# Two attention layers on one core: the shift cut as columns, a whole-array product in the last two stages, and the parts of attn and v spread over three engines

## The chip, the cores and the metric

One core of one Trainium2 chip. The time is device microseconds of one execution, and lower is better. Engines: PE (matmul), DVE (vector), ACT (activation), POOL (GpSimd), and SP, which only issues DMAs here.

## The reference

Two self-attention layers over x of 4 images, 128 channels and 1024 positions (32 x 32). For each image of each layer:

```python
q = Wq @ x + bq            # 16 x 1024
k = Wk @ x + bk            # 16 x 1024
v = Wv @ x + bv            # 128 x 1024
attn = softmax(q.T @ k, over the last axis)     # 1024 x 1024
x = gamma * (v @ attn.T) + x
```

The second layer takes the output of the first. Everything is fp32.

## The kernel before

A **stage** is one image in one layer: stages 0 to 3 are the four images of layer 0, and 4 to 7 those of layer 1. Stage s + 4 needs the x of stage s. All stages run the same steps, overlapped:

- **QK.s** (`project_qk`, L502): PE projects q and k, three copies over one another, into a ring tile. DVE makes two operations of it, `mask` (L403) and `stack` (L410): in `qk` some copies hold the rounded fp32r value and one the rest, so that one fp32r pass over 64 rows gives q.k closely. SP then copies the halves of `qk` crosswise into `qk_swapped` (`swap`, L265). Stage 0 starts from fp32 q and k directly (`qk_raw`).
- **E.s.i** (L525): a tile of 128 rows of q.T @ k, 1024 wide, as two matmuls on the upper and the lower 64 rows of the array at once. DVE takes the negated row maximum (`max`, L433), and ACT makes exp(e - max) with the row sum (`sum`, L341).
- **The shift** -(max + ln(sum)) belongs to each row. ACT copies the maxima and takes the logarithm (`log_sums`, L347). PE transposes both with two fp32 products (`transpose_shift`, L540), DVE splits the result into a rounded row and the rest (`shift_to_rows`, `rows`, L438), and SP writes these rows into `qk` and `qk_swapped` by two DMAs (`place`, L271). Stage 0 does this in two halves of four tiles, the others once.
- **ET.s.k** (L550): the transposed energies with the shift already in them, and ACT's exp of them is the finished `attn` (L356).
- **Parts.** fp32 x fp32 on PE costs more than fp32r passes do. For six of the eight tiles k (1 to 6), `attn` is cut into `attn_hi` (rounded to fp32r) and `attn_lo` (the rest), and likewise `v` into `v_hi` and `v_lo`. Tiles 0 and 7 are native: fp32 as it is.
- **V.s** (L514) projects v, DVE adds the bias (`v32`, L418).
- **Product** out = v @ attn: PH.s.k is v_hi and v_lo times attn_hi (four passes), PV.s.k is v_hi times attn_lo (two passes) or the native product. Each pass is a pair of matmuls (`add_product`, L564) on 64 rows of the array each: the upper rows write bank 0 of `out_psum`, the lower ones bank 1. k below 4 makes the first 512 positions, the others the second 512. `finish` (L455) adds both banks with gamma onto x, in two DVE operations for each half, and only then may the next half use the banks (`wait_for_out`, L574).

PSUM holds `out_psum` and a ring of three tiles, which raw, QK, E, shift, ET and V share. The order of every engine's work is written out by hand as lists of names (PE_ORDER, L34, and the like), whose last number on PE is the ring tile. A semaphore wait stands ahead of each use, so an engine stops at an item that isn't ready, and all behind it waits too. Where PE would idle, `warm` products of zeros stand. An attn slot k is free once the earlier stage's `lo` of this k is made (or its product, for native tiles).

Who does what before: POOL makes all 48 `lo` and 32 of the `hi`, ACT 16 `hi` and all 8 `v_hi`, DVE all 8 `v_lo`.

Of the kernel before, what the change touches and what calls it, by code (L numbers as in the profile page):

```python
# [72 lines left out]
rows.1.1 mask.3.0 max.2.0 stack.3.0 finish.0.0 max.2.7 max.2.1 max.2.5 max.2.3 v_lo.1.0 max.3.7 max.3.5 finish.0.1
v32.2.0 max.3.1 max.3.4 rows.2.1 max.3.3 max.3.0 mask.4.0 stack.4.0 finish.1.0 max.3.2 max.3.6 v_lo.2.0 max.4.4
max.4.7 finish.1.1 rows.3.1 max.4.3 max.4.6 mask.5.0 stack.5.0 max.4.0 max.4.5 max.4.2 max.4.1 finish.2.0 max.5.0
v32.3.0 max.5.1 v_lo.3.0 finish.2.1 rows.4.1 max.5.5 max.5.7 max.5.2 max.5.3 max.5.4 finish.3.0 mask.6.0 stack.6.0
v32.4.0 v_lo.4.0 max.5.6 max.6.3 finish.3.1 v32.5.0 rows.5.1 max.6.0 max.6.7 max.6.5 max.6.1 finish.4.0 v_lo.5.0
# [595 lines left out]
```

## Time and profile before

| | us |
|---|---|
| median of 3 runs | 207.81 (207.34 to 209.48) |
| profiled execution | 206.91 |
| its span | 205.0 |
| PE busy | 192.7 (94%) |
| ACT busy | 161.0 (79%) |
| POOL busy | 155.9 (76%) |
| DVE busy | 144.8 (71%) |

PE's busy time is from modelled ends, which overlap the next matmul; starts tell more. One slice of forty is 5.1 us. The granted clock is 1.0 (2.4 GHz) in most of the span; in slices 4 and 5 it is 0.8 and 0.5.

### The profile page before, as it was taken

The numbers are of one execution on the slowest core, as the hardware profiler recorded it, in microseconds if no ns is written. First come the engines' busy times: TensorE is split into PE (matmuls) and PEld (weight loads), VectorE is DVE, ScalarE is ACT, GpSimd is POOL, SyncE is SP. The second block draws the span as 40 slices with busy tenths as digits, with TensorE's granted clock in tenths as the row PEclk, the third lists the DMA queues.
The fourth block names the chain that finished last, engine by engine and source line by source line (L and its number), as shares of the span: only waits on it lengthen the run. The fifth ranks groups of instructions, "written<-read, shape, count | busy, mean of one in ns | idle before, by whom it ended". The sixth has DMA issues, their size and how long they took to land.

```text
span 205.0 us, 3349 instructions
## 1 busy us (share of the span) xinstructions
PE 192.7 (94%) x1217; PEld 124.8 (61%) x1217; DVE 144.8 (71%) x146; ACT 161.0 (79%) x237; POOL 155.9 (76%) x88
## 2 busy tenths in 40 slices
PE   7999999999889998999999999999999899998792
PEld 2433254555578656647875867775676768777570
DVE  0297688996999789689866897879874876532202
ACT  2229659889999989997999979699979997558420
POOL 1330000686499999998978988999999999999990
PEclk9998599999999999999999999999999999999998
DMA  6808000030040004002100004001410101001011
GB/s 184 328 14 205 0 2 3 13 93 0 3 106 0 2 6 102 0 6 51 51 3 3 0 2 107 0 6 51 102 53 5 51 0 51 30 28 51 3 51 51
DMA packets 3746, 9.31 MB, mean 45 GB/s; under 512 B 532, under 2 KB 916, under 8 KB 3732
## 3 DMA queue, kind: packets, MB, share of 16 engines
q1 hardware_dynamic: 3732, 9.12, 15.0%
q8 instruction: 10, 0.16, 0.3%
q14 instruction: 4, 0.03, 0.1%
HBM read 2.69 MB, written 2.10 MB: 23 GB/s over the span
## 4 chain that ended last, share of the span: by engine, by line
PE 51%; ACT 15%; POOL 15%; DVE 9%; issue 6%; DMA 2%; SPq 0%; POOLq 0%; DVEq 0%; ACTq 0%
PE out_psum L570 20%; POOL attn_lo L310 10%; PE ring L535 8%; ACT ring L344 7%; ACT attn L362 6%; PE out_psum L600 5%; POOL attn_hi L305 4%; PE out_psum L571 4%; DVE neg_max L435 4%; PE ring L521 4%; PE ring L511 3%; PE ring L556 3%; DMA qk_swapped<-qk 2%; PE ring L499 2%; DVE x_all L460 1%
## 5 line engine op out<-in xcount | busy, mean ns | idle before, releaser
L310 POOL TENSOR_TENSOR attn_lo<-attn,attn_hi 128x1024 fp32r<-128x1024 f32 x48 | 116.2, 2441 | 8.9 <-ACT attn_hi L369 8.0
L435 DVE TENSOR_REDUCE neg_max<-ring 128x1 f32<-128x1024 f32 x64 | 76.5, 1220 | 14.3 <-PE ring L537 13.5
L344 ACT ACTIVATE ring<-ring,neg_max 128x1024 f32<-128x1024 f32 x64 | 69.7, 1088 | 13.1 <-DVE neg_max L435 12.4
L362 ACT ACTIVATE attn<-ring 128x1024 f32<-128x1024 f32 x64 | 63.5, 1024 | 15.8 <-PE ring L558 15.4
L305 POOL TENSOR_SCALAR attn_hi<-attn 128x1024 fp32r<-128x1024 f32 x32 | 36.2, 1138 | 27.9 <-ACT attn L362 27.4
L556 PE MATMUL ring<-qk,qk_swapped 64*128 64x512 f32 x64 | 30.1, 485 | 2.7 <-ACT attn L362 2.0
L570 PE MATMUL out_psum<-attn_hi,v_hi 64*128 64x512 f32 x96 | 30.7, 399 | 1.5 <-DVE x_all L463 1.2
L571 PE MATMUL out_psum<-attn_hi,v_hi 64*128 64x512 f32 x96 | 30.7, 399 | 0.0
L558 PE MATMUL ring<-qk_swapped,qk 64*128 64x512 f32 x64 | 30.5, 491 | 0.0
L570 PE MATMUL out_psum<-attn,v 64*128 64x512 f32 x64 | 30.0, 588 | 0.0
L571 PE MATMUL out_psum<-attn,v 64*128 64x512 f32 x64 | 30.0, 588 | 0.0
L571 PE MATMUL out_psum<-attn_hi,v_lo 64*128 64x512 f32 x96 | 29.6, 388 | 0.0
L570 PE MATMUL out_psum<-attn_hi,v_lo 64*128 64x512 f32 x96 | 29.6, 388 | 0.0
L570 PE MATMUL out_psum<-attn_lo,v_hi 64*128 64x512 f32 x96 | 28.2, 400 | 0.1
L571 PE MATMUL out_psum<-attn_lo,v_hi 64*128 64x512 f32 x96 | 28.2, 400 | 0.0
L535 PE MATMUL ring<-qk_swapped,qk 64*128 64x512 f32 x56 | 24.7, 445 | 2.4 <-ACT attn L362 2.2
L460 DVE SCALAR_TENSOR_TENSOR x_all<-out_psum,weights,x_all 128x512 f32<-128x512 f32 x16 | 12.0, 748 | 20.2 <-PE out_psum L571 20.2
L537 PE MATMUL ring<-qk,qk_swapped 64*128 64x512 f32 x56 | 25.0, 448 | 0.0
L556 PEld LDWEIGHTS ring<-qk,qk_swapped 64*128 64x128 f32 x64 | 11.7, 184 | 14.0 <-issue 12.6
L570 PEld LDWEIGHTS out_psum<-attn_hi,v_hi 64*128 64x128 f32 x96 | 17.0, 184 | 5.0 <-issue 2.7
L570 PEld LDWEIGHTS out_psum<-attn_lo,v_hi 64*128 64x128 f32 x96 | 17.5, 184 | 3.5 <-POOL attn_lo L310 1.0
L570 PEld LDWEIGHTS out_psum<-attn_hi,v_lo 64*128 64x128 f32 x96 | 17.7, 184 | 2.3
(48 smaller groups left out, 322.4 us busy)
## 6 DMA issues: line engine op xcount, KB each, us to landing
qk_swapped<-qk SPq DMA_DIRECT2D x16, 256.0 KB, 3.7
out_dram<-x_all SPq DMA_DIRECT2D x8, 256.0 KB, 2.0
x_all<-x_in SPq DMA_DIRECT2D x3, 512.0 KB, 7.1
x_all<-x_in SPq DMA_DIRECT2D x2, 256.0 KB, 3.2
late<-late_in SPq DMA_DIRECT2D x1, 448.0 KB, 6.3
weights<-weights_in SPq DMA_DIRECT2D x1, 132.0 KB, 2.1
qk<-shift_rows SPq DMA_DIRECT2D x7, 8.0 KB
qk_swapped<-shift_rows SPq DMA_DIRECT2D x7, 8.0 KB
```

The source lines that it names most:

```text
L305: nc.gpsimd.tensor_scalar(attn_hi[:, k - 1], attn[:, k], 1.0, 0.0, ALU.mult, ALU.add).then_inc(hi_made["gpsimd"], 1)
L310: nc.gpsimd.tensor_tensor(attn_lo[:, k - 1], attn[:, k], attn_hi[:, k - 1].bitcast(fp32), ALU.subtract).then_inc(lo_made, 1)
L344: nc.scalar.activation(e[:], e[:], ACT.Exp, bias=max_column(s, i), accum_out=row_sum[s][:, i:i + 1]).then_inc(sum_made, 1)
L362: nc.scalar.activation(attn[:, k], ring_tile("ET", s, k)[:].rearrange("p (a n) -> p a n", a=2), ACT.Exp).then_inc(attn_made, 1)
L435: nc.vector.tensor_reduce(max_column(s, i), ring_tile("E", s, i)[:], axis=AX.X, op=ALU.max, negate=True).then_inc(max_made, 1)
L460: nc.vector.scalar_tensor_tensor(out=to, in0=out_psum[:, 0:HALF], scalar=gamma, in1=x_all[:, s, part], op0=ALU.mult, op1=ALU.add).then_inc ...
L535: nc.tensor.matmul(to[:, 0:HALF], q_over_k[0:deep, rows], k_over_q[0:deep, 0:HALF], start=True, stop=True)
L537: nc.tensor.matmul(to[:, HALF:N], k_over_q[64:64 + deep, rows], q_over_k[64:64 + deep, HALF:N], start=True, stop=True).then_inc(e_mm, 1)
L556: nc.tensor.matmul(to[:, 0:HALF], k_over_q[0:64, first], q_over_k[0:64, part], start=True, stop=True)
L558: nc.tensor.matmul(to[:, HALF:N], q_over_k[64:128, second], k_over_q[64:128, part], start=True, stop=True).then_inc(et_mm, 1)
L570: nc.tensor.matmul(out_psum[:, 0:HALF], v[0:64], a[0:64], start=start, stop=stop)
L571: last = nc.tensor.matmul(out_psum[:, HALF:N], v[64:128], a[64:128], start=start, stop=stop)
```

## The change

- **Shift.** `log_sums` makes only the logarithm of 4 or 8 sums; the copy of the maxima goes. A new DVE item `parts` (`cut_shift`) makes three small operations of 128 x 4 or 128 x 8 in SBUF: shift = neg_max - log_sum, its rounded value, and the rest. PE transposes these 8 or 16 columns by one fp32r product with a unit matrix. `rows` is one DVE copy out of PSUM. SP's two DMAs stay as they are. `ADDED`, a way without these DMAs, is empty: its branches run in no stage; only two POOL memsets of 128 x 128 remain of it.
- **Product.** In stages 6 and 7 (`WHOLE`) each pass is one matmul on all 128 rows, which writes the bank of its half; `finish` is then one DVE operation a half, and a half waits only for the same bank's last finish.
- **Stage 1's stack** goes from DVE to ACT (`evac`) and POOL (mask and stack from SBUF).
- **Parts:** POOL 38 `lo`, 32 `hi`, 6 `v_hi`, 6 `v_lo`; ACT 16 `hi`, 2 `v_hi`; DVE 10 `lo` (two in stage 3, one in 5, three in 6, four in 7) and 2 `v_lo`.
- **Loads:** `late` has 5 tiles of 64 KB instead of 7. A new load `units` of 5 such tiles stands ahead of the last two x, and POOL rounds it (one operation of 128 x 640).
- **All five orders are new.** PE has 26 `warm` instead of 31.

```diff
+WHOLE = (6, 7)
+FROM_SBUF = (1,)
...
 PE_ORDER = """
-raw.0.0.0 raw.0.1.1 QK.1.0.2 E.0.2.0 E.0.1.1 warm.0.8 E.0.0.2 E.0.3.0 warm.0.2 E.0.4.1 warm.0.1 E.0.5.2 E.0.7.0
-warm.0.2 E.1.6.1 warm.0.3 E.1.4.2 warm.0.3 shift.0.0.0 warm.0.2 E.1.7.1 warm.0.1 E.0.6.0 V.0.0.2 ET.0.3.1 warm.0.1
...
+raw.0.0.0 raw.0.1.1 QK.1.0.2 E.0.1.0 E.0.3.1 E.0.6.2 warm.0.4 E.0.0.0 E.0.2.1 E.0.5.2 warm.0.2 E.0.4.0 warm.0.1
+V.0.0.1 shift.0.0.2 warm.0.2 E.0.7.0 E.1.7.1 QK.2.0.2 warm.0.4 ET.0.2.0 warm.0.1 ET.0.3.1 warm.0.3 E.1.3.0 ET.0.1.2
...
+shift.7.1.0 PV.6.0 ET.6.7.1 ET.6.4.2 ET.6.1.0 PH.6.5 PH.6.3 PV.6.2 PV.6.5 ET.7.0.2 ET.7.2.0 ET.7.7.1 PH.6.1 PV.6.7
+ET.7.3.2 ET.7.5.0 PV.6.1 PV.6.3 PH.6.4 PH.6.6 ET.7.1.2 ET.7.4.1 ET.7.6.0 PV.6.4 PV.6.6 PH.7.3 PH.7.2 PV.7.7 PH.7.1
+PV.7.2 PV.7.3 PV.7.1 PV.7.0 PH.7.5 PH.7.6 PH.7.4 PV.7.5 PV.7.4 PV.7.6
 ACT_ORDER = """
-sum.0.2 sum.0.1 sum.0.0 sum.0.3 log.0.0 sum.0.4 sum.0.5 sum.0.7 sum.1.6 sum.1.4 sum.1.7 sum.0.6 attn.0.3 log.0.1
...
+evac.1.0 sum.0.1 sum.0.3 sum.0.6 sum.0.0 sum.0.2 sum.0.5 log.0.0 sum.0.4 v_hi.0.0 sum.0.7 sum.1.7 attn.0.2 log.0.1
...
+sum.7.1 attn.5.5 attn.5.7 hi.5.5 sum.7.4 sum.7.7 sum.7.0 attn.6.2 attn.6.5 sum.7.5 log.7.1 attn.6.6 attn.6.0
+attn.6.3 hi.6.3 attn.6.4 attn.6.1 attn.6.7 v_hi.7.0 attn.7.0 attn.7.2 hi.6.6 hi.7.2 attn.7.3 attn.7.7 attn.7.5
+attn.7.1 attn.7.4 hi.7.5 attn.7.6 hi.7.4 hi.7.6
 DVE_ORDER = """
-mask.1.0 max.0.2 stack.1.0 max.0.1 max.0.0 max.0.3 max.0.4 max.0.5 max.0.7 max.1.6 max.1.4 rows.0.0 max.1.7 max.0.6
...
+max.0.1 max.0.3 max.0.6 max.0.0 max.0.2 max.0.5 max.0.4 parts.0.0 v32.0.0 rows.0.0 max.0.7 max.1.7 mask.2.0
...
+parts.7.1 v32.7.0 lo.6.2 rows.7.1 lo.6.1 lo.6.3 finish.6.0 finish.6.1 lo.7.3 lo.7.1 lo.7.6 lo.7.5 finish.7.0
 finish.7.1
 POOL_ORDER = """
...
+mask.1.0 stack.1.0 v_lo.0.0 hi.0.2 hi.0.1 hi.0.3 lo.0.2 lo.0.1 hi.0.6 lo.0.3 lo.0.6 hi.0.5 lo.0.5 hi.0.4 lo.0.4
...
+v_lo.7.0 lo.6.4 lo.6.6 hi.7.3 hi.7.1 lo.7.2 lo.7.4
...
             def log_sums(s, h):
-                act.wait_ge(max_made, all_of(nth_max, s, tiles))
-                nc.scalar.copy(neg[:, len(tiles):], neg[:, 0:len(tiles)]).then_inc(max_twice, 1)
                 act.wait_ge(sum_made, all_of(nth_sum, s, tiles))
-                sums = row_sum[s][:, tiles.start:tiles.stop][:, None, :].to_broadcast([P, 2, len(tiles)])
-                nc.scalar.activation(log, sums, ACT.Ln).then_inc(log_made, 1)
+                nc.scalar.activation(log_sum[s][:, part], row_sum[s][:, part], ACT.Ln).then_inc(log_made, 1)
...
+            def cut_shift(s, h):
...
+                dve.wait_ge(max_made, all_of(nth_max, s, tiles))
+                dve.wait_ge(log_made, nth_log[s, h])
+                nc.vector.tensor_tensor(shift[s][:, part], neg_max[s][:, part], log_sum[s][:, part],
+                                        ALU.subtract).then_inc(shift_made, 1)
+                dve.wait_ge(shift_made, nth_parts[s, h])
+                nc.vector.tensor_copy(hi, whole).then_inc(shift_hi_made, 1)
+                dve.wait_ge(shift_hi_made, nth_parts[s, h])
+                nc.vector.tensor_tensor(lo, whole, hi.bitcast(fp32), ALU.subtract).then_inc(shift_cut, 1)
...
             def shift_to_rows(s, h):
-                nc.vector.tensor_scalar(shift_masked[0:rows], src, columns[0:rows, mask:mask + 1], None,
-                                        ALU.mult).then_inc(shift_masked_made, 1)
-                nc.vector.tensor_tensor(shift_rows[s % 2][0:rows], src, shift_masked[0:rows].bitcast(fp32),
-                                        ALU.subtract).then_inc(shift_in_rows, 1)
+                nc.vector.tensor_copy(rows_of(s, h)[:], ring_tile("shift", s, h)[0:rows, 0:P]
+                                      ).then_inc(shift_in_rows, 1)
...
+            def attn_lo_of(s, k):
+                wait_for_cut(dve, "hi", s, k)
+                nc.vector.tensor_tensor(attn_lo[:, k - 1], attn[:, k], attn_hi[:, k - 1].bitcast(fp32),
+                                        ALU.subtract).then_inc(cut_made["lo", "vector"], 1)
...
             def finish(s, h):
+                if s not in WHOLE:
+                    nc.vector.scalar_tensor_tensor(out=to, in0=out_psum[:, 0:HALF], scalar=gamma, in1=x,
+                                                   op0=ALU.mult, op1=ALU.add).then_inc(x_half_made, 1)
...
+                bank, x = (out_psum[:, part], x) if s in WHOLE else (out_psum[:, HALF:N], to)
...
             def transpose_shift(s, h):
-                nc.tensor.matmul(to, both(neg_max, s, h), late[:, IDENTITY], start=True, stop=False)
-                nc.tensor.matmul(to, both(log_sum, s, h), late[:, IDENTITY + 1], start=False,
-                                 stop=True).then_inc(shift_mm, 1)
+                nc.tensor.matmul(to, parts, units[:, IDENTITY], start=True, stop=True).then_inc(shift_mm, 1)
...
                 for n, (v, a) in enumerate(passes):
...
+                    if s in WHOLE:
+                        last = nc.tensor.matmul(out_psum[:, half_of(k)], v, a, start=start, stop=stop)
```

## Rows read from the trace of the kernel before

**Rows 1.** Stretches: bounds, us, busy us of each engine, granted clock, DMA share, GB/s.

```profile
18.00:26.00 8.00, 8.00 (x23) 2.21 (x21) 5.29 (x5) 6.15 (x13) 0.00 (x0) 0.57 0.23 55
...
38.00:175.00 137.00, 132.49 (x918) 93.27 (x919) 111.53 (x112) 126.99 (x189) 125.52 (x67) 1.00 0.12 32
...
sum 205.00, PE 192.69 PEld 124.75 DVE 144.76 ACT 161.01 POOL 155.92; mean PE 32.12 PEld 20.79 DVE 24.13 ACT 26.84 POOL 25.99
```

**Rows 2.** The chain that ended last, from the page: shares of the span.

```profile
PE 51%; ACT 15%; POOL 15%; DVE 9%; issue 6%; DMA 2%; SPq 0%; POOLq 0%; DVEq 0%; ACTq 0%
```

**Rows 3.** Waits: engine and line, what it waited for, total us, times, longest.

```profile
DVE x_all L460 <- PE out_psum L571: 20.2, 11, 6.6
```

**Rows 4.** Groups by form: busy us, mean ns | idle us ahead of them, releasers.

```profile
L310 POOL TENSOR_TENSOR attn_lo<-attn,attn_hi 128x1024 fp32r<-128x1024 f32 x48 | 116.2, 2441 | 8.9 <-ACT attn_hi L369 8.0
...
L435 DVE TENSOR_REDUCE neg_max<-ring 128x1 f32<-128x1024 f32 x64 | 76.5, 1220 | 14.3 <-PE ring L537 13.5
...
L344 ACT ACTIVATE ring<-ring,neg_max 128x1024 f32<-128x1024 f32 x64 | 69.7, 1088 | 13.1 <-DVE neg_max L435 12.4
...
L362 ACT ACTIVATE attn<-ring 128x1024 f32<-128x1024 f32 x64 | 63.5, 1024 | 15.8 <-PE ring L558 15.4
...
L305 POOL TENSOR_SCALAR attn_hi<-attn 128x1024 fp32r<-128x1024 f32 x32 | 36.2, 1138 | 27.9 <-ACT attn L362 27.4 <-PE out_psum L571 0.5
...
L369 ACT CAST attn_hi<-attn 128x1024 fp32r<-128x1024 f32 x16 | 16.7, 1046 | 0.2
...
L374 ACT CAST v_hi<-v 128x768 fp32r<-128x768 f32 x8 | 6.6, 829 | 0.0
...
L446 DVE TENSOR_SCALAR shift_masked<-ring,weights 16x128 fp32r<-16x128 f32 x7 | 2.3, 334 | 5.3 <-PE ring L547 5.3
```

**Rows 5.** Timeline of stage 0: start us, us, engine, line, instruction, idle before.

```profile
19.23 0.21 ACT L354 ACTIVATE log_sum<-row_sum 128x8 f32<-128x8 f32 x1
...
26.24 0.39 PE L546 MATMUL ring<-late,neg_max 128*8 128x128 f32 x2
...
31.11 0.50 PE L556 MATMUL ring<-qk,qk_swapped 64*128 64x512 f32 x1
...
31.65 1.02 ACT L362 ACTIVATE attn<-ring 128x1024 f32<-128x1024 f32 x1
...
37.02 2.06 POOL L305 TENSOR_SCALAR attn_hi<-attn 128x1024 fp32r<-128x1024 f32 x2 [25.06 <-ACT attn L362]
```

**Rows 6.** Timeline of POOL and DVE around two `v_lo`.

```profile
123.71 2.41 POOL L310 TENSOR_TENSOR attn_lo<-attn,attn_hi 128x1024 fp32r<-128x1024 f32 x1 [1.72 <-ACT attn_hi L369]
...
124.41 2.53 DVE L430 TENSOR_TENSOR v_lo<-v,v_hi 128x768 fp32r<-128x768 f32 x1 [1.09 <-ACT v_hi L374]
...
140.62 0.95 DVE L430 TENSOR_TENSOR v_lo<-v,v_hi 128x768 fp32r<-128x768 f32 x1
```

**Rows 7.** Timeline of PE from a projection of 128 rows to pairs of 64.

```profile
139.26 1.98 PE L511 MATMUL ring<-x_all,late 128*128 128x512 f32 x4
...
141.18 0.50 PE L556 MATMUL ring<-qk,qk_swapped 64*128 64x512 f32 x1
...
141.51 0.39 PE L570 MATMUL out_psum<-attn_hi,v_hi 64*128 64x512 f32 x1
...
141.75 0.39 PE L570 MATMUL out_psum<-attn_hi,v_hi 64*128 64x512 f32 x1
```

**Rows 8.** Timeline of stage 7's shift on PE, and of V.7.0.

```profile
174.73 0.39 PE L546 MATMUL ring<-late,neg_max 128*16 128x128 f32 x2
...
176.53 2.05 PE L521 MATMUL ring<-late,x_all 128*128 128x128 f32 x16
```

**Rows 9.** Timeline of the end: POOL's last parts, PE's last pair, DVE's last.

```profile
193.12 7.05 POOL L310 TENSOR_TENSOR attn_lo<-attn,attn_hi 128x1024 fp32r<-128x1024 f32 x3
...
200.56 0.39 PE L571 MATMUL out_psum<-attn_lo,v_hi 64*128 64x512 f32 x1
...
201.79 0.75 DVE L463 SCALAR_TENSOR_TENSOR x_all<-out_psum,weights,x_all 128x512 f32<-128x512 f32 x1
```

More of the change, by code:

```diff
@@ L73 @@
[L73 to L77, printed above, removed]
@@ L78 @@
-mask.7.0 stack.7.0 max.6.6 max.6.2 max.6.4 finish.4.1 rows.6.1 v32.6.0 max.7.1 max.7.6 finish.5.0 max.7.4 v_lo.6.0
-max.7.0 max.7.3 finish.5.1 max.7.5 max.7.2 max.7.7 rows.7.1 finish.6.0 v32.7.0 v_lo.7.0 finish.6.1 finish.7.0
+max.0.1 max.0.3 max.0.6 max.0.0 max.0.2 max.0.5 max.0.4 parts.0.0 v32.0.0 rows.0.0 max.0.7 max.1.7 mask.2.0
+stack.2.0 parts.0.1 max.1.3 rows.0.1 max.1.2 max.1.6 max.1.1 max.1.5 max.1.4 max.1.0 max.2.5 parts.1.1 v32.1.0
+max.2.2 rows.1.1 max.2.3 max.2.0 finish.0.0 mask.3.0 stack.3.0 max.2.7 max.2.6 max.2.1 max.2.4 max.3.3 max.3.2
@@ new lines @@
+finish.0.1 v32.2.0 parts.2.1 max.3.4 rows.2.1 max.3.0 max.3.7 mask.4.0 max.3.6 stack.4.0 finish.1.0 max.3.5 max.3.1
+max.4.5 max.4.1 max.4.0 finish.1.1 max.4.4 parts.3.1 max.4.3 rows.3.1 max.4.2 max.4.7 mask.5.0 stack.5.0 max.4.6
+finish.2.0 parts.4.1 v32.3.0 max.5.3 max.5.1 max.5.4 max.5.7 rows.4.1 finish.2.1 v32.4.0 lo.3.1 max.5.0 lo.3.6
+max.5.5 finish.3.0 max.5.2 max.5.6 mask.6.0 stack.6.0 v_lo.4.0 parts.5.1 finish.3.1 v32.5.0 rows.5.1 mask.7.0
+max.6.0 stack.7.0 max.6.1 max.6.4 finish.4.0 max.6.2 max.6.6 max.6.3 max.6.5 v_lo.5.0 max.6.7 finish.4.1 max.7.6
@@ L80 @@
+v32.6.0 parts.6.1 max.7.2 max.7.3 max.7.1 finish.5.0 rows.6.1 max.7.4 max.7.7 max.7.0 lo.5.5 max.7.5 finish.5.1
+parts.7.1 v32.7.0 lo.6.2 rows.7.1 lo.6.1 lo.6.3 finish.6.0 finish.6.1 lo.7.3 lo.7.1 lo.7.6 lo.7.5 finish.7.0
 finish.7.1
@@ L325, in _ @@
                     attn_hi_of(s, k)
+                elif what == "lo":
+                    attn_lo_of(s, k)
+                elif what == "v_hi":
+                    make_v_hi(s)
+                elif what == "v_lo":
+                    make_v_lo(s)
+                elif what == "mask":
+                    mask_from_sbuf(s)
                 else:
-                    attn_lo_of(s, k)
+                    stack_from_sbuf(s)
         @block.scalar
@@ L384, in _ @@
                     make_v_hi(s)
+                elif what == "evac":
+                    evacuate_qk(s)
                 else:
@@ L438, in shift_to_rows @@
             def shift_to_rows(s, h):
-                rows = 2 * len(tiles_of(s, h))
-                mask = HALF_SHIFT_MASK if s in BY_HALVES else SHIFT_MASK
-                src = ring_tile("shift", s, h)[0:rows, 0:P]
+                rows = P if added(s, h) else 2 * len(tiles_of(s, h))
                 dve.wait_ge(shift_mm, nth_shift[s, h])
-                earlier = [use[1:3] for use in DVE_USES if use[0] == "rows" and nth_rows[use[1:3]] < nth_rows[s, h]]
-                if earlier:
-                    dve.wait_ge(shift_in_rows, nth_rows[earlier[-1]])
@@ L476, in _ @@
                     make_v_lo(s)
+                elif what == "lo":
+                    attn_lo_of(s, i)
+                elif what == "parts":
+                    cut_shift(s, i)
                 elif what == "rows":
@@ L653 @@
         late[:, BV + l] = bv_l[None, :]
-    late[:, IDENTITY] = np.eye(P, dtype=f32)
-    late[:, IDENTITY + 1] = -late[:, IDENTITY]
+    units = np.zeros((P, UNITS, P), f32)
+    units[:, IDENTITY] = np.eye(P, dtype=f32)
+    for t in range(SLOTS):
+        for row in (t, SLOTS + t):
+            units[[row, 64 + row], SELECT + t] = 1.0
     late[:, LAYER1] = sets[QK_SETS]
```

307 lines of the change are left out of this document (188 added, 119 removed).

## The prediction

> **What bounds the kernel now.** I read the chain of waits first: PE has 51% of it, ACT and POOL 15% each, DVE 9% [rows 2]. No engine is the bound alone. The busy times say why [rows 1]: from 38 to 175 us, with the clock at 2.4 GHz, ACT is busy for 127.0 of 137.0 us, POOL for 125.5, DVE for 111.5. PE shows 132.5, but modelled ends flatter it, so I count it by starts. A pair of fp32r matmuls of 512 columns starts 0.23 us after the one ahead, a set of four fp32 halves takes 1.92 [rows 7], a V 1.98 [rows 8]. With the counts of the order, E and ET cost 0.23 each, PH 0.92, a cut PV 0.46, a native PV 1.92, QK 1.92, V 1.98, a stage 0 E 0.96, a shift 0.32, a `warm` 0.23. Between the shifts 0.1 (about 37 us) and 7.1 (174.7 us) [rows 8] stand 126.6 us of this, so PE is idle for about 10 us there. All four engines have some 19 us a stage; an engine that is relieved gives back only waits.
>
> **The start** is slack. In stage 0 the logarithm of the first half starts at 19.23, but PE comes to its shift at 26.24, behind E tiles and warm products; the first ET is at 31.11, the first attn at 31.65, POOL's first `hi` at 37.02 [rows 5]. From 18 to 26 us the granted clock is 0.57, mostly the 1.2 GHz level [rows 1].
>
> **The end** is POOL's. After the shift of stage 7 PE has 23.2 us of work and takes 26.2 us for it (174.73 to 200.95) [rows 8, 9]; POOL makes `lo` without a gap until 200.17, the last pair follows, then two halves of a finish. DVE waits 20.2 us in all for PE's products [rows 3].
>
> **The change, part by part.**
>
> *Start.* Log.0.0 now stands behind six sums instead of four: two tiles more at DVE's 1.2 us [rows 4]. DVE loses the mask and stack of stage 1, two operations on a tile, of which I credit one (1.2). So the log ends at about 20.6, `parts` takes 0.5, and shift to ET is 4.9 us as now [rows 5]: ET at 26.0, attn at 26.5, 5.1 us earlier. ACT has 11.9 us behind it then and not 12.2, but 1.1 of it is the new `evac`, so about 1 us is owed: **-4.0**. Stage 1's q and k pass from POOL: rounding the units 0.7, mask 1.0, stack 2.35 (like a `lo`, 7.05/3) [rows 9]. They end some 2 us later than now, ahead of an E.1 first wanted beyond 21: nothing, and 2 us if the cover is gone. The load adds 0.32 MB and `late` loses 0.13 MB: it delays images 2 and 3, not wanted before QK.2; nothing.
>
> *Order on PE.* From shift.0.1 up to shift.7.1 the new order has 124.8 us of PE work instead of 126.6 (three ET and two PH fewer, one V more, among others): **-1.8**.
>
> *Relief of ACT and POOL in the middle.* From the first attn to log.7.1 ACT had 131.9 us and has 121.3: 6 `v_hi` (0.83), the copies, and attn and `hi` moved behind it [rows 4]. POOL has from its first `hi` 38 x 2.35 + 32 x 1.03 + 6 x 0.77 + 5 x 1.76 = 135.7 us (the last two are `hi` and `lo` scaled to 768 columns) instead of 145.8 [rows 5, 9]. PE's 10 us of idle time can shrink by at most this: between 0 and -5 I take **-2.0**, since DVE doesn't get lighter (141.5 to 143.8 without waits).
>
> *Parts on DVE.* The trace shows what DVE pays when both inputs lie in SBUF: `v_lo` takes 0.95 us with POOL between operations and 2.53 when it starts 0.7 us into a `lo` of POOL, which is the rest of that operation and then itself [rows 6]. Ops with one PSUM input (the max, 1.22) don't show this. A `lo` on DVE is 0.95 x 1024/768 = 1.27 plus a rest. The mean rest of POOL's mix is (38 x 2.35² + 32 x 1.03²) / (2 x 122.3) = 1.0 us. Ten make 22.7 on DVE, and hold POOL for 12.7 against 23.5 saved; the six `v_lo` gone give back 5.7. For SBUF the Trainium skill says the same and more (SBUF — State Buffer, section SBUF: two separate sides): the two engines share a port pair under an exclusive lock, and it also binds a DVE copy in a 2-port mode. By that rule the new copy in `parts` would wait as well.
>
> *Shift.* Gone from the chain from log to ET: one ACT copy (0.18, ahead of the log) and one small DVE operation (0.33) [rows 4]; new: three of at most 0.2 us each in `parts`, both ends in SBUF. If they run together behind one rest, 1.0 + 0.5 a stage; if POOL gets in between each time, 1.0 + 2 x 1.76 (POOL's mean operation) + 0.5 = 5.0. No small operation with two SBUF inputs is in the trace, so both ends stay open. I take the one wait, nearest to the `v_lo` rows, and a third of seven of them exposed, since ACT holds 6 to 12 us of other work behind each log: 7 x 1.0 / 3 = **+2.3**, less 0.3 for the lighter transpose: **+2.0**. Queued behind `parts` on DVE are maxima, which ACT's sums and the ring wait for.
>
> *Whole array and tail.* A full-array pass streams the same 512 columns: 1.92/4 for each fp32 half [rows 7]; nothing gained a pass. Changing between 64-row and 128-row work costs 0.1 us: the pair after the switch is followed 0.33 and not 0.24 us later [rows 7]. Stages 6 and 7 have 14 changes instead of 7: +0.7. On such switches TensorEngine Tiling (Array Packing) in the Trainium skill, Tiling Modes, says that a change of mode drains the engine; the trace agrees, at this 0.1. Behind shift.7.1 PE has 26.2 us of work instead of 23.2; POOL has only four operations of stage 7 and is no bound. With 1.5 us idle: 26.2 + 0.7 + 1.5 = 28.4 instead of 26.2, and the last finish is one operation: -0.75 [rows 9]. Together **+1.4**. ACT has 21.1 us behind log.7.1, then two DVE `lo`, PV, finish: about 25, inside it.
>
> **Sum:** -4.0 - 1.8 - 2.0 + 2.0 + 1.4 = -4.4. The profiled execution was 206.91 (its span 205.0 and 1.9 around it): 202.5. The median is 0.9 above: **203.4**.
>
> **Rivals.**
>
> *DVE is held behind POOL (slower).* Place: `parts` in stages 1 to 7. Each costs 5.0, i.e. 4.5 of waiting; a third exposed is 10.5 instead of 2.3, so 203.4 + 8.2 = **211.6**. DVE would be busy for 143.8 + 31.5 + 10 = 185 us of some 190. It decides from about 2.9 us of waiting each: then a third of seven is the 6.7 us that the rest gains. For it: all-busy POOL and the 2.53 row [rows 1, 6]; by the named SBUF page the copy waits too. Against it: DVE's next operation may start before POOL's. Chance 0.18.
>
> *PE has the same work (no change).* In all it has 173.7 us instead of 174.9. If what the start wins is lost later at the ring or in DVE's list, only 1.2 remains: **206.6**. For it: ACT's attn slots are free only when `lo` is made, DVE's `lo` come late in its list, finish.7.0 now stands behind lo.7.5, and the start can fall into the low clock. Chance 0.22.
>
> *The waits go (more gain).* PE's idle in the middle shrinks by 5, no `parts` is exposed: 203.4 - 3 - 2 = **198.4**. Against it: DVE and ACT are fed by the same three ring tiles. Chance 0.13.
>
> *The forecast* has 0.47; its own range is 201 to 206.
>
> **Numbers.** 1% is about 2.1 us, which is what can be told from no change: below 205.7 is faster, above 209.9 slower. Faster: 0.13, 0.42 of the forecast and 0.03 of the no-change case, 0.58. Slower: 0.16 of the rival and 0.03 of others, 0.19. Same: 0.23. The range 198.0 to 210.0 leaves out a tail of the third rival and most of the slower one.
>
> **What would show it.** First attn at 26 to 27 us. `parts` operations: 0.2 us each with one of about 1 us, or several of 1 to 2.4 us. DVE's `lo` at 1.3 to 3.6 us. POOL idle in the last 10 us. PE's pace in stages 6 and 7: a pass each 0.23 us; if 128-row fp32r passes came slower, the 72 cut passes of these stages would add 1.4 us for each 0.02. The prediction is wrong if attn starts no earlier than 30 us, or if DVE is busy for more than 170 us.

## The result: 7.6% slower, and all of it comes with the three small operations of the shift

| | before | after |
|---|---|---|
| median | 207.57 us (4 runs) | 223.63 us (222.56 to 225.16, 4 runs) |
| ratio to before | | 1.0763 [1.0667, 1.0859] |
| profiled execution, its span | 206.91, 205.0 | 223.82, 222.0 |
| PE, ACT, POOL, DVE busy | 192.7, 161.0, 155.9, 144.8 | 196.8, 156.5, 153.5, 171.5 |
| granted clock, mean | 0.978 | 0.939 |

PE and POOL are busy for about as long as before, ACT for 4.5 us less. DVE has 26.7 us more than before. The first view is the page of the kernel after: the granted clock in 40 slices, and the chain that ended last, by engine and by line [rows 2 for before].

```profile
PEclk9995799985999889999999999979999769999999
...
PE 52%; DVE 16%; POOL 13%; ACT 10%; issue 7%; DVEq 0%; ACTq 0%; POOLq 0%
PE out_psum L694 12%; PE ring L645 8%; POOL attn_lo L348 8%; PE out_psum L692 6%; PE ring L621 6%; ACT attn L447 5%; ACT ring L435 5%; DVE shift_parts L544 5%; PE out_psum L728 5%; PE out_psum L695 5%; DVE shift L541 4%; PE ring L669 4%; PE ring L631 3%; DVE neg_max L526 3%; DVE v L511 2%
```

DVE's share rose from 9% to 16%. Two lines on 128 x 8 numbers, L541 and L544, have 9% of the chain, about 20 us. The groups by form say what they cost (mean ns of one behind the busy time):

```profile
L521 DVE TENSOR_TENSOR attn_lo<-attn,attn_hi 128x1024 fp32r<-128x1024 f32 x10 | 20.2, 2049 | 4.8 <-POOL attn_hi L343 4.8
...
L544 DVE CAST shift_parts<-shift 128x8 fp32r<-128x8 f32 x7 | 10.5, 1502 | 0.2
...
L541 DVE TENSOR_TENSOR shift<-neg_max,log_sum 128x8 f32<-128x8 f32 x7 | 9.0, 1289 | 0.6 <-ACT log_sum L442 0.3
...
L546 DVE TENSOR_TENSOR shift_parts<-shift,shift_parts 128x8 fp32r<-128x8 f32 x7 | 4.7, 674 | 0.2
```

The three take 24.2 us in seven stages, from 0.5 us in stage 4 to 5.2 us in stage 1. What they take alone is seen in stage 4, where POOL happens to be idle. The timelines of the kernel after, first DVE's in stages 2 and 4 (start, duration):

```profile
70.07 0.90 DVE L541 TENSOR_TENSOR shift<-neg_max,log_sum 128x8 f32<-128x8 f32 x1
71.01 2.29 DVE L544 CAST shift_parts<-shift 128x8 fp32r<-128x8 f32 x1
73.33 0.75 DVE L546 TENSOR_TENSOR shift_parts<-shift,shift_parts 128x8 fp32r<-128x8 f32 x1
74.00 1.21 DVE L526 TENSOR_REDUCE neg_max<-ring 128x1 f32<-128x1024 f32 x1
...
110.01 0.17 DVE L541 TENSOR_TENSOR shift<-neg_max,log_sum 128x8 f32<-128x8 f32 x1
110.22 0.17 DVE L544 CAST shift_parts<-shift 128x8 fp32r<-128x8 f32 x1
110.42 0.17 DVE L546 TENSOR_TENSOR shift_parts<-shift,shift_parts 128x8 fp32r<-128x8 f32 x1
```

and POOL's over the same two moments:

```profile
66.23 7.03 POOL L348 TENSOR_TENSOR attn_lo<-attn,attn_hi 128x1024 fp32r<-128x1024 f32 x3
73.23 0.84 POOL L354 TENSOR_SCALAR v_hi<-v 128x768 fp32r<-128x768 f32 x1
...
104.43 2.38 POOL L348 TENSOR_TENSOR attn_lo<-attn,attn_hi 128x1024 fp32r<-128x1024 f32 x1
111.42 1.06 POOL L343 TENSOR_SCALAR attn_hi<-attn 128x1024 fp32r<-128x1024 f32 x1 [4.62 <-ACT attn L447]
```

POOL's three `lo` end at 68.59, 70.95 and 73.27, and `v_hi` at 74.07. DVE's three operations end at 70.97, 73.30 and 74.08. So each of them waits for one whole operation of POOL or its rest. The reading, which e5 tests below, is this: in the 0.03 us between two of DVE's, where it waits for its own semaphore, POOL's next operation gets in.

Who waited for whom, in the kernel after:

```profile
POOL attn_hi L343 <- ACT attn L447: 36.3, 11, 10.2
ACT attn L447 <- PE ring L671: 23.6, 16, 5.1
ACT ring L435 <- DVE neg_max L526: 19.0, 15, 4.3
...
PE ring L657 <- DVE shift_parts L546: 5.7, 3, 2.5
```

PE's own wait at the shift is only 5.7 us. The chain that ended last nevertheless goes through the small operations in six of the seven stages, all but stage 4, and leaves them by what stands next in DVE's list: a maximum in stages 2, 3 and 6, V's bias (`v32`) in 1 and 7, a `finish` in 5. The pieces of the chain in stage 2 (start, us, what) show the way by a maximum:

```profile
68.94 1.21 DVE v L511
70.15 0.83 DVE shift L541
...
71.01 2.30 DVE shift_parts L544
...
74.00 1.22 DVE neg_max L526
...
76.26 0.20 ACT ring L435
...
76.60 1.19 PE ring L621
```

DVE is through with `parts` at 74.1, takes the maximum that was queued behind it, ACT takes the sum of that ring tile, and only then is the tile free for PE's next projection.

The span, cut at PE's shifts of stage 0's second half and of stage 7 (us; e1 and e8 are experiments below):

| | start to shift.0.1 | from there to shift.7.1 | to the end | span |
|---|---|---|---|---|
| before | 36.20 | 138.53 | 30.27 | 205.0 |
| after | 32.09 | 159.00 | 30.91 | 222.0 |
| e1, shift as before | 31.72 | 137.32 | 31.46 | 200.5 |
| e8, parts on POOL | 30.93 | 137.37 | 30.90 | 199.2 |

The start is gained, the end is nearly what it was, and the middle has 20.5 us more. In the middle stretch the granted clock is 0.94 in the kernel after and 1.00 in the other three, and PE is busy for 139.0 us with 886 matmuls where e8 needs 130.4 for 888: up to 8.6 us of the loss may be matmuls at the lower clock, which came with the waits.

One profile, of e2, is of a disturbed execution, so only durations of single operations are taken from it.

### The profile page after: what moved, and what is told of

Its sections match the earlier page's. It is cut to its first block, busy times and chain, and to the rows that moved or that the text cites. A ratio compares the mean times of both kernels' runs of the same rounds, so it can differ in the third digit from the quotient of the medians.

```text
span 222.0 us, 3109 instructions
## 1 busy us (share of the span) xinstructions
PE 196.8 (89%) x1095; PEld 123.4 (56%) x1097; DVE 171.5 (77%) x162; ACT 156.5 (71%) x223; POOL 153.5 (69%) x95
## 4 chain that ended last, share of the span: by engine, by line
PE 52%; DVE 16%; POOL 13%; ACT 10%; issue 7%; DVEq 0%; ACTq 0%; POOLq 0%
PE out_psum L694 12%; PE ring L645 8%; POOL attn_lo L348 8%; PE out_psum L692 6%; PE ring L621 6%; ACT attn L447 5%; ACT ring L435 5%; DVE shift_parts L544 5%; PE out_psum L728 5%; PE out_psum L695 5%; DVE shift L541 4%; PE ring L669 4%; PE ring L631 3%; DVE neg_max L526 3%; DVE v L511 2%
## 5 line engine op out<-in xcount | busy, mean ns | idle before, releaser
L348 POOL TENSOR_TENSOR attn_lo<-attn,attn_hi 128x1024 fp32r<-128x1024 f32 x38 | 94.9, 2517 | 3.8 <-ACT attn_hi L453 3.2
L447 ACT ACTIVATE attn<-ring 128x1024 f32<-128x1024 f32 x64 | 63.3, 1026 | 24.4 <-PE ring L671 23.6
L343 POOL TENSOR_SCALAR attn_hi<-attn 128x1024 fp32r<-128x1024 f32 x32 | 33.3, 1049 | 39.3 <-ACT attn L447 36.3
L645 PE MATMUL ring<-qk_swapped,qk 64*128 64x512 f32 x56 | 26.5, 483 | 1.2 <-ACT attn L447 0.4
L647 PE MATMUL ring<-qk,qk_swapped 64*128 64x512 f32 x56 | 26.7, 487 | 0.0
L694 PE MATMUL out_psum<-attn_hi,v_hi 64*128 64x512 f32 x72 | 23.8, 411 | 0.3 <-POOL attn_hi L343 0.3
L521 DVE TENSOR_TENSOR attn_lo<-attn,attn_hi 128x1024 fp32r<-128x1024 f32 x10 | 20.2, 2049 | 4.8 <-POOL attn_hi L343 4.8
L695 PE MATMUL out_psum<-attn_hi,v_hi 64*128 64x512 f32 x72 | 23.8, 411 | 0.0
L694 PE MATMUL out_psum<-attn,v 64*128 64x512 f32 x48 | 23.6, 614 | 0.0
L695 PE MATMUL out_psum<-attn,v 64*128 64x512 f32 x48 | 23.6, 614 | 0.0
L694 PE MATMUL out_psum<-attn_hi,v_lo 64*128 64x512 f32 x72 | 22.9, 398 | 0.0
L695 PE MATMUL out_psum<-attn_hi,v_lo 64*128 64x512 f32 x72 | 22.9, 397 | 0.0
L694 PE MATMUL out_psum<-attn_lo,v_hi 64*128 64x512 f32 x72 | 21.9, 409 | 1.1 <-POOL attn_lo L348 1.1
L669 PEld LDWEIGHTS ring<-qk,qk_swapped 64*128 64x128 f32 x64 | 11.7, 191 | 19.4 <-issue 17.8
L695 PE MATMUL out_psum<-attn_lo,v_hi 64*128 64x512 f32 x72 | 21.9, 408 | 0.0
L360 POOL TENSOR_TENSOR v_lo<-v,v_hi 128x768 fp32r<-128x768 f32 x6 | 11.5, 1922 | 10.9 <-ACT v_hi L458 10.8
L631 PEld LDWEIGHTS ring<-late,x_all 128*128 128x128 f32 x128 | 16.7, 209 | 2.4 <-issue 2.4
L631 PE MATMUL ring<-late,x_all 128*128 128x128 f32 x128 | 17.9, 299 | 0.0
```

The lines of the kernel that those rows point to most:

```text
L343: nc.gpsimd.tensor_scalar(attn_hi[:, k - 1], attn[:, k], 1.0, 0.0, ALU.mult, ALU.add).then_inc(cut_made["hi", "gpsimd"], 1)
L348: nc.gpsimd.tensor_tensor(attn_lo[:, k - 1], attn[:, k], attn_hi[:, k - 1].bitcast(fp32), ALU.subtract).then_inc(cut_made["lo", "gpsimd"], 1)
L447: nc.scalar.activation(attn[:, k], ring_tile("ET", s, k)[:].rearrange("p (a n) -> p a n", a=2), ACT.Exp).then_inc(attn_made, 1)
L631: last = nc.tensor.matmul(to[:, j * C:(j + 1) * C], x_all[:, s, j * P:(j + 1) * P], late[:, WV + layer(s), :], start=True, stop=True)
L645: nc.tensor.matmul(to[:, 0:HALF], q_over_k[0:deep, rows], k_over_q[0:deep, 0:HALF], start=True, stop=True)
L647: nc.tensor.matmul(to[:, HALF:N], k_over_q[64:64 + deep, rows], q_over_k[64:64 + deep, HALF:N], start=True, stop=True).then_inc(e_mm, 1)
```

## The experiments

Four theories stood at first. LOCK: the small operations wait for POOL, and that is the loss. CLOCK: gaps on PE let the granted clock fall, and that costs. ORDER: the new orders cost. WHOLE: the whole-array product costs. The kernel before took 207.59 us beside e1 to e4, 207.41 beside e5 to e8 and 206.99 beside e9 to e12; each ratio is to the one that ran beside.

**e1: the kernel after with the shift of before.** All the rest of the change stays.

```
-                nc.vector.tensor_tensor(shift..., neg_max..., log_sum..., ALU.subtract)
-                nc.vector.tensor_copy(hi, whole)
-                nc.vector.tensor_tensor(lo, whole, hi.bitcast(fp32), ALU.subtract)
+                nc.scalar.copy(neg[:, len(tiles):], neg[:, 0:len(tiles)])     # on ACT
+                (two products on PE, mask and subtraction from PSUM on DVE)
```

> The changed kernel with the shift made as before the change: ACT's copy of the maxima, two fp32 transposes on PE, two DVE operations out of PSUM, and no `parts` on DVE. All orders, the whole-array product and the spread of hi and lo stay as changed. Theory LOCK (the three small DVE operations of `parts` wait for POOL's running operation, 24.3 us of DVE time in stages 1 to 7, and hold the shift and the maxima behind them): at least 13 of the 16 us come back, 206 to 211 us, and ACT, POOL and PE lose most of their idle time in the middle. Rival ORDER (the new lists and the tail are worse by themselves): at most 5 us come back, 218 us or more. Rival WHOLE (128-row passes and their mode changes): as ORDER, with the loss behind the shift of stage 6.

Measured 202.77 us, ratio 0.9791 [0.9745, 0.9837]. The whole loss, 223.63 - 202.77 = 20.9 us, sits in the new shift; the rest of the change is worth 2.1%. That is more than the 13 to 18 us that I had expected back. ACT's waits for DVE's maxima fall from 19.0 to 8.2 us, those for PE from 23.6 to 11.7, and the chain's shares (page) are:

```profile
PE 56%; POOL 25%; ACT 11%; issue 5%; DVE 1%; POOLq 0%; ACTq 0%
```

DVE has left the chain.

**e2: the kernel before with the new shift alone.** `parts` is put into DVE's list of before, in each stage between the logarithm's last maximum and `rows`.

```
+ dve: shift = neg_max - log_sum; hi = copy(shift); lo = shift - hi      (in words)
+ pool: the unit matrix is rounded once
- act: copy of the maxima;  pe: two fp32 products  ->  one fp32r product
```

> The kernel before with the new shift alone: `parts` on DVE one item ahead of `rows` in DVE's list (right ahead of `rows` in stage 7), logarithm without the copy, one fp32r transpose. All else as before. LOCK: the operations wait for POOL here too, some 3 us a stage; 7 stages give 215 to 225 us. ORDER and WHOLE: the shift is not to blame, 207 to 210 us.

Measured 233.1 us, ratio 1.1222 [1.1152, 1.1292]: some 25 us without any of the new orders, and more than the 215 to 225 us expected. The three operations take 6.6, 9.1 and 8.2 us there, 23.9 together. The new orders are not to blame. That they hide a little of the cost (20.9 us in the kernel after) is a guess: `parts` stands in other places of DVE's list here.

**e3: the kernel before with the whole-array product alone.**

```
+WHOLE = (6, 7)
+ if s in WHOLE: last = nc.tensor.matmul(out_psum[:, half_of(k)], v, a, ...)
```

> The kernel before with the whole-array product of stages 6 and 7 alone (one matmul of 128 rows a pass into the bank of its half, one DVE operation for each half of a finish). LOCK: no part in the loss, 206 to 208.5 us: two finishes shorter by 0.75 us on the path at the end, some 0.1 us lost at each change of mode. WHOLE: 211 us or more.

Measured 207.42 us, ratio 1.0 [0.9976, 1.0024]. Neutral, as LOCK had it.

**e4: the kernel after with 12 small products of zeros ahead of PE's wait at the shift** of stages 1 to 7, so that PE is not idle there.

```
+                if s > 0:
+                    for _n in range(12):
+                        nc.tensor.matmul(ring_tile("shift", s, h)[:, 0:HALF], zeros[:, 0:P], zeros[:], ...)
```

> The changed kernel with 12 more products of zeros on PE ahead of the wait for each shift of stages 1 to 7, into the ring tile that the shift owns by then (about 2.8 us of PE time each, where PE mostly waits). Rival CLOCK (the loss is the granted clock, 0.939 instead of 0.978, once PE idles): the clock returns to 0.97 and 4 to 8 us come back, 216 to 219 us. LOCK: the waits stay; the time changes by no more than 3 us either way, since the products also take PE time where it had none to give: 221 to 228 us.

Measured 226.94 us, ratio 1.0948 [1.0905, 1.0991]. Span and granted clock of the core:

```profile
core 0: 225.3 us, clock 0.977
```

The clock is back at the level of before (0.978), and the kernel is still slower than the one after by 3.3 us: the 4 to 8 us that CLOCK promised did not come back. Part of that is the products themselves: 84 at 0.23 us are 19 us of PE, of which only some lie in gaps (DVE's `rows` now wait 11.8 us for PE). So the run does not price the clock, and it shows only that keeping the clock up in this way wins nothing. Where no small operation of DVE waits (e1, e7, e8) the clock is 0.99; that the gaps which DVE makes bring the fall is read from this, and not shown by itself.

**e5: the second operation made from the same inputs as the first,** so that no semaphore wait stands between them.

```
+                nc.vector.tensor_tensor(hi, neg_max[s][:, part], log_sum[s][:, part], ALU.subtract)
-                dve.wait_ge(shift_made, nth_parts[s, h])
-                nc.vector.tensor_copy(hi, whole)
```

> The changed kernel, but the rounded part of the shift is made from neg_max and log_sum by a tensor_tensor of its own, right behind the first one and with no wait between the two; the third operation waits for both. Same number of DVE operations, same values. Theory GAP (POOL's next operation starts in the gap that a semaphore wait leaves between two small DVE operations, and each gap costs one more wait of 1.0 to 2.4 us): the second operation takes 0.2 us, DVE is busy some 8 us less, and a third of the 20.9 us that `parts` costs comes back, 214 to 219 us. Rival EACH (every small operation waits, gap or none): the second still shows about 1.5 us and the time stays at 222 to 226 us.

Measured 216.64 us, ratio 1.0449 [1.0382, 1.0516]: 7.0 us back. DVE's timeline in stage 2 of e5, to set against the one above:

```profile
69.97 0.94 DVE L541 TENSOR_TENSOR shift<-neg_max,log_sum 128x8 f32<-128x8 f32 x1
70.83 0.15 DVE L543 TENSOR_TENSOR shift_parts<-neg_max,log_sum 128x8 fp32r<-128x8 f32 x1
71.08 2.15 DVE L547 TENSOR_TENSOR shift_parts<-shift,shift_parts 128x8 fp32r<-128x8 f32 x1
```

The second operation follows at once and takes 154 ns in the mean of seven instead of 1502; the third, behind a wait, now meets the whole POOL operation and rises from 674 to 1397 ns. POOL's next `lo` starts at 70.83 too and does not hold the second operation up. That one is now a subtraction and not a copy, but the first and the third are subtractions too and do wait. So it is the wait at a semaphore that lets POOL in. DVE was relieved of 4.5 us and not of the 8 expected, since the third operation took over part of the waiting; these 4.5 us gave 7.0 us of time, a third of the 20.9, as expected.

**e6 and e7: the disputed cost by itself.** To e1, three chained small operations are added ahead of `mask` in stages 2 to 7. Nothing of the kernel uses their results. In e6 all inputs are in SBUF; in e7 one input of each is the ring tile in PSUM.

```
+                src = weights[:, 0:8]                    # e6;   e7: ring_tile("QK", s, 0)[:, 0:8]
+                nc.vector.tensor_tensor(small[0][:], src, weights[:, 8:16], ALU.subtract)
+                nc.vector.tensor_copy(small[1][:], small[0][:])          # e7: copies src
+                nc.vector.tensor_tensor(small[2][:], src, small[1][:], ALU.subtract)
```

> The kernel with the old shift and all the rest of the change (202.8 us), plus three small DVE operations of 128 x 8 ahead of each `mask` of stages 2 to 7, chained by waits as in `parts`, on columns of `weights` in SBUF; their outputs go to scratch. They stand on no shift's chain. Theory LOCK: each waits for POOL's running operation; about 3 us a stage of DVE time, 18 in all. If what costs is DVE being held (maxima and sums late), the time goes to 209 to 218 us; if what costs is the late shift alone, it stays below 206 us.

> As the run with small operations in SBUF, in the same places, but the first input of each of the three comes from the ring tile in PSUM, so none has two inputs in SBUF and the copy is from PSUM. LOCK: no waits for POOL; each takes 0.2 to 0.3 us, 5 us of DVE time in all, 202.5 to 205 us. Rival COUNT (it is the number of small chained operations that costs, wherever the inputs lie): the same time as with SBUF inputs.

Groups of e6:

```profile
L512 DVE TENSOR_TENSOR small<-weights,small 128x8 f32<-128x8 f32 x6 | 9.4, 1567 | 0.2
L510 DVE COPY small<-small 128x8 f32<-128x8 f32 x6 | 8.3, 1378 | 0.2
...
L508 DVE TENSOR_TENSOR small<-weights 128x8 f32<-128x8 f32 x6 | 4.5, 752 | 1.0 <-PE ring L628 1.0
```

Groups of e7:

```profile
L510 DVE COPY small<-ring 128x8 f32<-128x8 f32 x6 | 1.0, 166 | 0.2
L512 DVE TENSOR_TENSOR small<-ring,small 128x8 f32<-128x8 f32 x6 | 1.0, 166 | 0.2
L508 DVE TENSOR_TENSOR small<-ring,weights 128x8 f32<-128x8 f32 x6 | 1.0, 162 | 0.9 <-PE ring L628 0.9
```

e6 took 232.99 us, ratio 1.1235 [1.118, 1.1289]; e7 206.33, ratio 0.994 [0.9906, 0.9973]. The same eighteen operations cost 30.2 us over e1 with all inputs in SBUF, and 3.6 us with one in PSUM. In e7 POOL had a `hi` or a `lo` under way beside five of the six groups, and none of the eighteen took over 168 ns. LOCK is shown, away from the chain of the shift, and the number of operations is not what costs. Both sizes were missed: I had expected 209 to 218 and 202.5 to 205. What went wrong is again the exposure: 19.2 us more on DVE (22.2 against 3.0) made 26.7 us of time. By the orders, `mask` and `stack` stand right behind these operations, and the waits of e6 show PE held there:

```profile
PE ring L677 <- DVE qk L521: 15.7, 5, 6.4
...
PE ring L638 <- DVE qk L521: 4.6, 1, 4.6
```

L521 is `stack`. PE waits 20.3 us for it, against 2.1 us in e7. The granted clock is 0.933 in e6 and 0.99 in e7; how much of the 26.7 us is the clock's was not shown.

**e8: the kernel after with the three operations on POOL.** `parts` stands in POOL's list near the place where the logarithm ends.

```
-                nc.vector.tensor_tensor(...)   nc.vector.tensor_copy(hi, whole)   nc.vector.tensor_tensor(...)
+                nc.gpsimd.tensor_tensor(...)   nc.gpsimd.tensor_scalar(hi, whole, 1.0, 0.0, ALU.mult, ALU.add)   nc.gpsimd.tensor_tensor(...)
```

> The changed kernel with the three operations of `parts` made by POOL instead of DVE, in POOL's list behind the operation that runs when the logarithm ends (by the trace of the run with the old shift). LOCK: POOL has no one to wait for but itself; the operations take 0.1 to 0.3 us each, the shift is late by at most the rest of one POOL operation, and the time is 202 to 207 us. ORDER or COUNT: no better than 218 us.

Measured **200.93 us**, ratio 0.9683 [0.9626, 0.974]: faster than before, 22.7 us faster than after, and 1 us below the range expected. Groups of e8 on POOL:

```profile
L393 POOL TENSOR_SCALAR shift_parts<-shift 128x8 fp32r<-128x8 f32 x7 | 2.4, 339 | 0.6
...
L390 POOL TENSOR_TENSOR shift<-neg_max,log_sum 128x8 f32<-128x8 f32 x7 | 1.5, 211 | 0.0
L395 POOL TENSOR_TENSOR shift_parts<-shift,shift_parts 128x8 fp32r<-128x8 f32 x7 | 1.4, 206 | 0.6
```

They cost POOL 5.3 us where they cost DVE 24.2. The middle one is long once, in stage 7 (timeline of e8, POOL then DVE):

```profile
166.71 1.16 POOL L393 TENSOR_SCALAR shift_parts<-shift 128x8 fp32r<-128x8 f32 x1
...
166.59 1.22 DVE L538 TENSOR_TENSOR attn_lo<-attn,attn_hi 128x1024 fp32r<-128x1024 f32 x1
```

Here the wait goes the other way: DVE's `lo` began first and POOL's small copy ends with it.

**e9: e8 with the first shift ahead of V.0.0 on PE, and `rows` ahead of `v32` on DVE.** In the kernel after, V.0.0 takes 3.62 us at the low clock and stands ahead of the shift.

```
-V.0.0.1 shift.0.0.2 warm.0.2 E.0.7.0 ...
+shift.0.0.2 V.0.0.1 warm.0.2 E.0.7.0 ...
```

> `parts` on POOL (200.9 us), and in stage 0 PE's shift.0.0 ahead of V.0.0, DVE's rows.0.0 ahead of v32.0.0. In the changed kernel V.0.0 runs at the low clock level for 3.6 us while the shift waits behind it, and the first attn starts at 29.4 us and not at the 26.5 of the prediction. If that V is what the start lacks: first attn at 26 to 27 us; if this reaches the end, 1 to 2 us come back, 199 to 200 us. If the start is covered by what follows: 200.5 to 201.5 us with the early attn.

Measured 205.26 us, ratio 0.9927 [0.9894, 0.9959]: 4.3 us slower than e8, a miss (199 to 201.5 expected). PE's timeline in e9:

```profile
20.25 0.39 PE L724 MATMUL out_psum<-zeros 128*128 128x512 bf16 x1
22.39 0.26 PE L653 MATMUL ring<-units,shift_parts 128*8 128x128 f32 x1 [1.74 <-POOL shift_parts L395]
22.65 3.75 PE L627 MATMUL ring<-late,x_all 128*128 128x128 f32 x16
...
31.61 0.50 PE L665 MATMUL ring<-qk,qk_swapped 64*128 64x512 f32 x1
```

and of e8:

```profile
20.14 3.24 PE L627 MATMUL ring<-late,x_all 128*128 128x128 f32 x16
23.13 0.30 PE L653 MATMUL ring<-units,shift_parts 128*8 128x128 f32 x1
...
28.07 0.50 PE L665 MATMUL ring<-qk,qk_swapped 64*128 64x512 f32 x1
```

The shift comes 0.7 us earlier, but PE waits for the parts with nothing to do, V starts 2.5 us later, and E.0.7, E.1.7 and QK.2, which stand ahead of the first ET, follow it. The first ET is 3.5 us later, and the first attn starts at 32.15 us and not at the 26 to 27 expected. From 20 to 30 us the clock is 0.66 in place of 0.86. V ahead of the shift was filling a wait.

**e10: e8 with DVE's three `lo` of stages 3 and 5 back on POOL.**

```
 DVE: -lo.3.1 -lo.3.6 -lo.5.5        POOL: +lo.3.1 +lo.3.6 +lo.5.5
```

> `parts` on POOL, and the three `lo` that DVE makes in stages 3 and 5 made by POOL instead, among its other `lo` of the stage. Theory LOCK: a `lo` takes POOL 2.35 us and DVE 1.22 us in which POOL stands too, so each of the three gives POOL some 1.1 us more and DVE 2 us less; POOL is the fullest engine there, so 1 to 3 us slower, 202 to 204 us. Rival: DVE's `lo` and its wait hurt the maxima more, and it gets faster, under 200 us.

Measured 206.65 us, ratio 0.9979 [0.9947, 1.0011]: 5.7 us worse than e8, in the direction expected and more than the 1 to 3 us. From 100 to 120 us POOL is full in both (19.41 and 19.42 us busy), but DVE has 10.14 us of work in place of 18.29, ACT 15.11 in place of 18.29, PE 17.58 in place of 18.92. The granted clock there is 0.91 in place of 1.00, which may be part of the 5.7 us. The likely reading is that everything waits behind the longer queue of POOL. These `lo` on DVE pay, lock and all.

**e11: e8 with all six `lo` of stage 7 on DVE,** so that POOL is idle beside them.

```
-finish.6.1 lo.7.3 lo.7.1 lo.7.6 lo.7.5 finish.7.0 finish.7.1            POOL: -lo.7.2 -lo.7.4
+finish.6.1 lo.7.2 lo.7.3 lo.7.1 lo.7.5 finish.7.0 lo.7.4 lo.7.6 finish.7.1
```

> `parts` on POOL, and all six `lo` of stage 7 on DVE (four before), POOL makes none. In the tail the `lo` of DVE and POOL take turns: DVE's four take 9.4 us. LOCK: two of POOL's 2.35 us each turn into 1.2 us on DVE, and no one waits for turns: 1.5 to 3 us faster, 198 to 199.5 us. If the two engines only seemed to take turns: DVE has two more operations and the end comes 1 to 2 us later.

Measured 200.86 us, ratio 0.9718 [0.9674, 0.9763]: level with e8, where 198 to 199.5 was expected. DVE's timeline in e8:

```profile
184.41 9.38 DVE L538 TENSOR_TENSOR attn_lo<-attn,attn_hi 128x1024 fp32r<-128x1024 f32 x4
```

and in e11:

```profile
183.64 5.01 DVE L538 TENSOR_TENSOR attn_lo<-attn,attn_hi 128x1024 fp32r<-128x1024 f32 x4
191.19 0.75 DVE L567 SCALAR_TENSOR_TENSOR x_all<-out_psum,weights,x_all 128x512 f32<-128x512 f32 x1 [2.54 <-PE out_psum L688]
```

Four `lo` take 5.01 us in place of 9.38, as LOCK has it. One by one, those of e8 take 1.62, 3.39, 3.38 and 1.21 us, and the two of POOL beside them 3.33 and 3.34: each engine's operation waits for the other's, turn by turn. Here POOL gets in though DVE's next operation shows no gap ahead of it; a semaphore wait stands there too, but one that was already met. The time was not there to be won: DVE then waits 2.54 us for PE, which ends the kernel.

**e12: e9 and e11 together.**

> Both of the last: the shift of stage 0 ahead of V, and all `lo` of stage 7 on DVE, with `parts` on POOL. If the two act in different places their gains add: 197 to 199 us.

Measured 204.32 us, ratio 0.9881 [0.9837, 0.9925], between e9 and e8 and not the 197 to 199 expected: neither part had a gain to add. The best versions are e8 and e11.

## Why the prediction was wrong

The forecast was 203.4 us, faster; it came out at 223.6. Of its two signs of being wrong one came: DVE is busy for 171.5 us, over 170 (the first attn starts at 29.37, under 30). Of the 20.2 us between them 18.9 are one term.

- **Shift, +2.0: this is the step that failed.** It measures +20.9 (after against e1), and both factors of the sum were mis-sized. *How many waits.* I took "the one wait, nearest to the `v_lo` rows", 1.0 + 0.5 us a stage. The seven stages took 24.2 / 7 = 3.5, of which 0.5 is the work and 3.0 waiting. The `v_lo` rows showed one operation of one wait; they could say nothing of three with a semaphore between each. *How much is exposed.* I took a third, since ACT had other work behind each logarithm. As much as all of it was: 20.7 us of waiting (24.2 - 7 x 0.5) made 20.9 us, of which up to 8.6 may be the lower clock that came with the waits. ACT had the work, but what stands behind `parts` in DVE's list was late too: in stage 2 a maximum, without which a ring tile did not come free (chain above), in other stages V's bias or a `finish`. I named that queue and gave it no price.
- **The slower rival had the mechanism and still fell short.** "DVE is held behind POOL" gave 5.0 us a stage and a third exposed, 211.6. Its point of decision, 2.9 us of waiting each, was just reached by the 3.0 measured. With full exposure its own price would have been 7 x 4.5 = 31.5 us. The argument against it, "DVE's next operation may start before POOL's", proved wrong in most stages, where DVE waits for a semaphore in between, and right where it does not (e5: 154 ns). It deserved far more than 0.18.
- **What the rule said.** The copy L544 took 1502 ns in the mean and 0.17 us with POOL idle, and with one input in PSUM the operations of e7 took 162 to 166 ns. The prediction quoted the Trainium skill (SBUF — State Buffer, section SBUF: two separate sides) on the exclusive lock of two engines over one port pair, and that a copy is bound by it too; the copy agrees. The same page of the Trainium skill, section Who interferes with whom, has it that a DVE instruction with at most one SBUF input outside those modes does not contend; e7 agrees. The rule was in hand, and was weighed as a single wait.
- **Start, -4.0.** At shift.0.1 the kernel after is 4.1 us ahead and e1 4.5: the number is right. The way there was not, so that this is partly luck: the first attn is at 29.37 and not at 26.5. The shift comes at 23.34 and not at about 21.1, since V.0.0 (3.62 us at the low clock) now stands ahead of it, and from there to the first ET it is 5.5 and not 4.9 us, with E.0.7, E.1.7 and QK.2 between.
- **Order -1.8 and middle -2.0.** Between the two shifts e1 takes 137.32 us in place of 138.53: -1.2 and not -3.8. The work that left ACT and POOL seems to have been mostly slack. The idle time of PE there was also read low: shift.0.1 stands at 36.20 and not at about 37, so PE had some 12 us to spare and not 10.
- **Whole array and tail, +1.4.** Behind shift.7.1 e1 takes 31.46 us in place of 30.27, +1.2: right, as far as the sum of the two goes. The pace held: in the kernel after the last passes of a whole bank start 0.23 us apart (timeline of PE):

```profile
215.69 0.39 PE L692 MATMUL out_psum<-attn_hi,v_hi 128*128 128x512 f32 x1
215.92 0.62 PE L692 MATMUL out_psum<-attn_hi,v_lo 128*128 128x512 f32 x2
216.38 0.62 PE L692 MATMUL out_psum<-attn_hi,v_hi 128*128 128x512 f32 x2
```

- **`lo` on DVE.** Ten took 20.2 us against 22.7 estimated. Four of them did not wait at all (1.21 to 1.23 us), the other six waited for the rest of an operation of POOL or for a whole one (1.62 to 3.40 us). On average that is one rest of 0.8 us each, near the 1.0 read from the `v_lo` row.
- **Sum without the shift.** Start, order, middle and tail gave -6.4, that is 203.4 - 2.0 = 201.4 us; e1, which has just these parts, took 202.8. 1.4 us of the miss are there.
- **No change and more gain.** Neither happened. e8 reaches 200.9, and it does so by taking DVE's waits away.

What stays open: why a microsecond of waiting on DVE costs 1.0 us of time in one kernel (after), 1.4 in e6 and 1.6 in e5's step. The fall of the granted clock (0.939 in after, 0.933 in e6, 0.991 in e1) is likely part of it, but no run here prices it alone.

## What to carry to other kernels

Beside a busy POOL, price a small operation on DVE with all its inputs in SBUF by the operation of POOL that it meets, and a chain of n of them with semaphores between by up to n such operations. Look for the one input that can come from PSUM (e7), put the chain on POOL itself (e8), or take semaphore waits out of it (e5). In an order written by hand, price a late operation by what is queued behind it on its own engine up to the resource that all engines share (here the three ring tiles), and expose it fully unless that path is shown to be slack.

## What the runs showed of the hardware

- A 128 x 8 operation on DVE took 0.15 to 0.17 us with POOL idle and up to 2.3 us beside a `lo` of POOL (2.29 in stage 2, up to 2.32 in e6), ending with POOL's operation.
- POOL got in at a semaphore wait between two operations of DVE, with 0.03 us between their records. Without that wait it did not: 154 ns in the mean of seven (e5).
- With one input in PSUM there was no wait: 162 to 166 ns beside the same work of POOL (e7, against 752 to 1567 in e6).
- `lo` side by side on DVE and POOL take turns: 3.4 us on DVE and 3.3 on POOL (e8), where they take 1.2 on DVE (e11) and 2.35 on POOL alone.
- A small operation of POOL waits for DVE in the same way: 1155 ns in place of some 200 (e8, stage 7).
